# Attention block with a spiking feed-forward: another order for maxima, V, statistics, one relu and the last tokens

## The reference

```
mod = (silu(c) @ wmod) split into sa, ca, ga, sb, cb, gb      # one row per batch
h   = layernorm(x) * (1 + ca) + sa
q, k, v = split(h @ qkv_w.T + qkv_b)                           # 16 heads of 8
q, k = rope(q), rope(k)
attn = softmax(causal(q @ k.T / sqrt(8)))
x   = x + ga * ((attn @ v) @ proj_w.T + proj_b)
h   = layernorm(x) * (1 + cb) + sb
y   = square(relu(h @ W_fc.T)) @ W_proj.T                      # 128 -> 512 -> 128
x   = x + gb * (number of spikes of 5 leaky steps driven by y) / 5
```

## Time and profile before

| | |
|---|---|
| median of the runs | 450.79 us (449.61 to 452.21) |
| the profiled execution | 447.9 us, its span 446.1 us |
| TensorE busy (matmul) | 389.0 us, 87% of the span |
| VectorE busy | 320.0 us, 72% |
| ScalarE busy | 263.3 us, 59% |
| GpSimd busy | 125.4 us, 28% |
| maxima (L955) | 368 reductions, 192.2 us |
| exponentials (L809) | 288, 163.5 us |

### The profile page before, as it was taken

The page is one execution under the profiler, slowest core; times in us unless marked ns, Lnnn a source line. Parts: engine busy times, 40 slices in busy tenths (PEclk is TensorE's granted clock), DMA queues, the critical chain, the costliest instruction groups (busy, mean ns, idle before and its releaser), DMA issues.

```text
span 446.1 us, 15629 instructions
## 1 busy us (share of the span) xinstructions
PE 389.0 (87%) x6603; PEld 251.9 (56%) x6603; DVE 320.0 (72%) x718; ACT 263.3 (59%) x459; POOL 125.4 (28%) x163
## 2 busy tenths in 40 slices
PE   3878989878999999998999989999999889888883
PEld 3326655545656665666557655666566646654653
DVE  6659987857884999478965998489956875631275
ACT  7203556576677666765686657766676558467522
POOL 7714211421341052403250244205340320040120
PEclk9989999999999999999999999999999999999999
DMA  6056463242424332232414241323224040011000
GB/s 212 24 159 168 110 203 107 67 128 70 113 60 114 77 101 79 92 95 49 137 62 133 54 135 60 110 62 96 79 82 106 25 137 17 16 38 28 3 24 25
DMA packets 26049, 38.53 MB, mean 86 GB/s; under 512 B 5796, under 2 KB 20716, under 8 KB 23692
## 3 DMA queue, kind: packets, MB, share of 16 engines
q1 hardware_dynamic: 25980, 37.53, 29.3%
HBM read 26.35 MB, written 8.65 MB: 78 GB/s over the span
## 4 chain that ended last, share of the span: by engine, by line
PE 42%; DVE 18%; DMA 12%; issue 9%; ACT 8%; SPq 6%; POOL 5%; ACTq 0%; POOLq 0%; DVEq 0%
PE o_bank L606 9%; PE d_bank L523 8%; PE t_bank L588 6%; DVE negmax L955 6%; PE s_bank L543 5%; DMA kf<-k_scr 3%; SPq L440 3%; ACT probs L809 3%; DVE xn L971 3%; PE a_bank L523 2%; DMA rden<-r_scr 2%; DMA r_scr<-rden_c 2%; DMA den<-o_raw 2%; PE t_bank L523 2%; SPq L444 2%
## 5 line engine op out<-in xcount | busy, mean ns | idle before, releaser
L955 DVE TENSOR_REDUCE negmax<-s_bank 128x1 f32<-128x512 f32 (+7 forms) x368 | 192.2, 565 | 66.3 <-PE s_bank L549 65.0
L809 ACT ACTIVATE probs<-t_bank 128x512 f32<-128x512 f32 x288 | 163.5, 595 | 87.5 <-PE t_bank L593 83.1
L543 PE MATMUL s_bank<-kf,qf 126*64 126x512 bf16 (+7 forms) x1024 | 118.5, 292 | 18.3 <-DVE negmax L955 15.4
L588 PE MATMUL t_bank<-qf,kf 128*64 128x512 bf16 (+7 forms) x1024 | 112.0, 288 | 10.2 <-ACT probs L809 8.9
L543 PEld LDWEIGHTS s_bank<-kf,qf 126*64 126x64 bf16 x1024 | 49.5, 109 | 50.4 <-DVE negmax L955 36.2
L606 PE MATMUL o_bank<-probs,v 128*32 128x512 f32 (+7 forms) x1024 | 75.2, 412 | 0.0
L549 PE MATMUL s_bank<-causal,identb 128*64 128x64 bf16 x1024 | 72.0, 194 | 0.0
L593 PE MATMUL t_bank<-causal_t,identb 128*64 128x64 bf16 x1024 | 64.4, 195 | 0.0
L588 PEld LDWEIGHTS t_bank<-qf,kf 128*64 128x64 bf16 x1024 | 41.2, 110 | 31.6 <-ACT probs L809 11.5
L593 PEld LDWEIGHTS t_bank<-causal_t,identb 128*64 128x64 bf16 x1024 | 47.6, 110 | 9.2
L549 PEld LDWEIGHTS s_bank<-causal,identb 128*64 128x64 bf16 x1024 | 46.6, 111 | 8.3 <-issue 8.2
(11 more groups left out here) (144 smaller groups left out, 441.6 us busy)
## 6 DMA issues: line engine op xcount, KB each, us to landing
qf<-q_scr SPq DMA_DIRECT2D x15, 576.0 KB
kf<-k_scr SPq DMA_DIRECT2D x45, 192.0 KB
q_scr<-parts SPq DMA_DIRECT2D x24, 128.0 KB, 1.7
k_scr<-parts SPq DMA_DIRECT2D x24, 128.0 KB, 1.7
xa<-in_x SPq DMA_DIRECT2D x8, 256.0 KB, 3.8
o_t<-o_raw SPq DMA_DIRECT2D x60, 32.0 KB, 2.2
rden<-r_scr SPq DMA_DIRECT2D x15, 128.0 KB
out_y<-count SPq DMA_DIRECT2D x7, 256.0 KB, 7.2
```

Of the source, the lines that this page charges most:

```text
L543: nc.tensor.matmul(bank[C * a:C * (a + 1), col:col + keys], qf[0:KS, slot, 2 * p + a, C * i:C * (i + 1)], kf[0:KS, slot, 2 * p + a, 0:keys ...
L588: nc.tensor.matmul(bank[C * a:C * (a + 1), col:col + w], kf[0:KX, slot, 2 * p + a, C * kb:C * (kb + 1)], qf[0:KX, slot, 2 * p + a, C * kb: ...
L809: nc.scalar.activation(probs[:, v, :], t_bank[u % 2][:, :], ACT.Exp, scale=SCALE).then_inc(e_done, 1)
L955: last = nc.vector.tensor_reduce(own[:, i, p:p + len(same)], cols, AX.X, ALU.max, negate=True)
```

## The change

Nothing is computed differently; operations stand in other places of the engines' lists.

- The maxima follow the table S_PACE, which repeats in each batch: two units in slots 0, 1, 27, 29, 32 and 34, one in all others. The sum of a batch (42) and the lead are as before.
- V of the next batch is made in slot 5 and copied in slot 6, not in 0 and 1.
- Statistics of the inputs move from slot 13 to slot 0, their normalisation from 17 to 3, and GpSimd's `deviation1` ahead of the split of half 2b + 1.
- In slot 32 ScalarE does the relu before the copy of the maxima's rows.
- At the end the token blocks are paired (0, 2) and (1, 3) instead of (0, 1) and (2, 3), so the first reciprocal needs 128 columns of all partitions and not 256; the products of the second pair come after the first residual. The first half's down projection begins before the second half's up projections are done, and ScalarE alternates relu and square for the second half.

```diff
--- before.py
+++ after.py
@@ -37,6 +37,8 @@
 RING = 3
 HALF = SEQ // 2
 
+LAST_TOKENS = ((0, 2), (1, 3))
+
 
 S_BANKS = []
 for first in (0, 2):
@@ -68,6 +70,9 @@
 S_START = 22
 S_RISE = 2
 
+S_PACE = [2, 2, 1, 1, 1, 1] + [1] * 21 + [2, 1, 2, 1] + [1, 2, 1, 2, 1]
+S_DONE = [sum(S_PACE[:at + 1]) for at in range(PER_BATCH)]
+
 
 
 PV_ORDER = (0, 1, 7, 2, 6, 3, 5, 4)
@@ -85,7 +90,7 @@
 Q_STORES = NPART
 
 
-A_AT = {-16: T1, -13: QK, -9: QK + 1, 0: V_}
+A_AT = {-16: T1, -13: QK, -9: QK + 1, 5: V_}
 
 D_AT = {16: PROJ, 25: T2, 27: FC, 29: FC + 1, 31: FC + 2, 33: FC + 3}
 Y_AT = {36: 0, 37: 1, 38: 2, 39: 3}
@@ -97,7 +102,8 @@
 
 
 def scores_ahead(u):
-    return min(NS * HALVES, -(-(u + 1) * NS // NU) + S_LEAD, S_START + S_RISE * (u + 1))
+    b, at = divmod(u, PER_BATCH)
+    return min(NS * HALVES, 2 * NS * b + S_DONE[at] + S_LEAD, S_START + S_RISE * (u + 1))
 
 
 def bank_at(u):
@@ -510,7 +516,7 @@
             store_out(final - 1)
             for part in range(2):
                 sp.wait_ge(last_y, part + 1)
-                sp.dma_start(out_t[final, :, 2 * part:2 * part + 2], y_last[:, 2 * part:2 * part + 2, :])\
+                sp.dma_start(out_t[final, :, part:NT:2], y_last[:, 2 * part:2 * part + 2, :])\
                     .then_inc(stored, 16)
             sp.wait_ge(stored, 16 * (NB + 1))
 
@@ -767,10 +773,10 @@
             pe.wait_ge(on_done, NB)
             pe.wait_ge(wo_gated, NB)
             for part in range(2):
-                pe.wait_ge(last_on, part + 1)
-                for t in (2 * part, 2 * part + 1):
-                    cols = slice(P * t, P * (t + 1))
-                    last = by_halves(last_projected[part], cols, o_n[:, cols], wo_g[:, final % 2, :])
+                pe.wait_ge(last_on, 2 * part + 2)
+                for j, t in enumerate(LAST_TOKENS[part]):
+                    last = by_halves(last_projected[part], slice(P * j, P * (j + 1)), o_n[:, P * t:P * (t + 1)],
+                                     wo_g[:, final % 2, :])
                 last.then_inc(last_proj, 1)
 
             pe.wait_ge(m_free, rows_made(HALVES - 1))
@@ -782,22 +788,34 @@
                     last = nc.tensor.transpose(last_turned[part][:, P * t:P * (t + 1)], xn2[:, t, :], ident[:, :])
                 last.then_inc(last_t2, 1)
                 keep_warm(t_bank[1], 256)
-            for part in range(2):
-                pe.wait_ge(last_h2, part + 1)
-                cols = slice(HALF * part, HALF * (part + 1))
-                for i in range(NF):
-                    if part == 1 and i == NF - 1:
-
-                        pe.wait_ge(last_relu, 2)
-                    by_halves(last_hidden[part][i], slice(0, HALF), wfc_sb[:, P * i:P * (i + 1)], h2T[:, cols])                        .then_inc(last_fc, 1)
-            for part in range(2):
-                for i in range(NF):
-                    pe.wait_ge(last_sq[part], i + 1)
-                    for t in (2 * part, 2 * part + 1):
-                        cols = slice(P * t, P * (t + 1))
-                        last = by_halves(last_results[part], cols, sq[:, i, cols], wpr_sb[:, i, :],
-                                         i == 0 and t == 2 * part, i == NF - 1 and t == 2 * part + 1)
-                last.then_inc(last_out, 1)
+
+            def last_up(part, i):
+                by_halves(last_hidden[part][i], slice(0, HALF), wfc_sb[:, P * i:P * (i + 1)],
+                          h2T[:, HALF * part:HALF * (part + 1)]).then_inc(last_fc, 1)
+
+            def last_down(part, i):
+                pe.wait_ge(last_sq[part], i + 1)
+                for t in (2 * part, 2 * part + 1):
+                    cols = slice(P * t, P * (t + 1))
+                    last = by_halves(last_results[part], cols, sq[:, i, cols], wpr_sb[:, i, :],
+                                     i == 0 and t == 2 * part, i == NF - 1 and t == 2 * part + 1)
+                if i == NF - 1:
+                    last.then_inc(last_out, 1)
+
+            pe.wait_ge(last_h2, 1)
+            for i in range(NF):
+                last_up(0, i)
+            last_down(0, 0)
+            pe.wait_ge(last_h2, 2)
+            last_up(1, 0)
+            for i in range(1, NF):
+                last_down(0, i)
+
+            pe.wait_ge(last_relu, 2)
+            for i in range(1, NF):
+                last_up(1, i)
+            for i in range(NF):
+                last_down(1, i)
 
         @block.scalar
         def _(act):
@@ -902,20 +920,23 @@
             for u in range(SLOTS):
                 n, v = divmod(u, NU)
                 b, at = divmod(u, PER_BATCH)
+                relus, squares = (RELU_LAST, SQUARE_LAST) if b == final else (RELU_AT, SQUARE_AT)
+
+                if v == M_AT + 1 and at in relus and b > 0:
+                    hidden(b - 1, relus[at])
                 if u == M_SECOND + 1:
                     first_maxima_out(1)
                 if v == M_AT + 1 and n + 1 < HALVES:
                     maxima_out(n + 1)
                 if v == 3 and n > 0:
                     outputs(n - 1)
-                if at == 1 and 0 < b < final:
+                if at == 6 and 0 < b < final:
                     place_values(b + 1)
                 if at - PER_BATCH == -15 and b + 2 < NB:
                     modulate1(b + 2)
                 if at == (24 if b == final else 26) and b > 0:
                     modulate2(b - 1)
-                relus, squares = (RELU_LAST, SQUARE_LAST) if b == final else (RELU_AT, SQUARE_AT)
-                if at in relus and b > 0:
+                if v != M_AT + 1 and at in relus and b > 0:
                     hidden(b - 1, relus[at])
                 exponentials(u)
                 if at in squares and b > 0:
@@ -934,10 +955,11 @@
                 cols = slice(HALF * part, HALF * (part + 1))
                 for i in range(NF):
                     act.wait_ge(last_fc, NF * part + i + 1)
-                    nc.scalar.activation(relu[:, i, cols], last_hidden[part][i][:, 0:HALF], ACT.Relu).then_inc(last_relu, 1)
-            for i in range(NF):
-                act.wait_ge(last_relu, NF + i + 1)
-                nc.scalar.activation(sq[:, i, HALF:SEQ], relu[:, i, HALF:SEQ], ACT.Square).then_inc(last_sq[1], 1)
+                    nc.scalar.activation(relu[:, i, cols], last_hidden[part][i][:, 0:HALF], ACT.Relu)\
+                        .then_inc(last_relu, 1)
+                    if part:
+                        act.wait_ge(last_relu, NF + i + 1)
+                        nc.scalar.activation(sq[:, i, cols], relu[:, i, cols], ACT.Square).then_inc(last_sq[1], 1)
 
         @block.vector
         def _(dve):
@@ -1121,9 +1143,9 @@
             for u in range(SLOTS):
                 b, at = divmod(u, PER_BATCH)
                 if b + 2 < NB:
-                    if at - PER_BATCH == -23:
+                    if at == 0:
                         statistics1(b + 2)
-                    if at - PER_BATCH == -19:
+                    if at == 3:
                         normalise1(b + 2)
                     if at - PER_BATCH in ROTARY_AT:
                         rotary(b + 2, *ROTARY_AT[at - PER_BATCH])
@@ -1151,24 +1173,31 @@
 
 
             parts_of = [(slice(HALF * part, HALF * (part + 1)), slice(2 * part, 2 * part + 2)) for part in range(2)]
+            inverse = rot_c[:, 0, 0:HALF]
             sums, raw = last_sums[:, 0:HALF], last_rows[:, 0:HALF]
-            inverse = rot_c[:, 0, 0:HALF]
-            dve.wait_ge(gathered, 1)
-            nc.vector.reciprocal(inverse, sums).then_inc(last_rden, 1)
             dve.wait_ge(on_done, final)
             dve.wait_ge(d_ready, before(final - 1, PROJ) + 1)
-            dve.wait_ge(gathered, 2)
-            dve.wait_ge(last_rden, 1)
-            for part, (cols, _) in enumerate(parts_of):
-                own = slice(C * part, C * (part + 1))
-                nc.vector.tensor_tensor(o_n[C:P, cols], raw[own, :], inverse[own, :], ALU.mult).then_inc(last_on, 1)
+
+            def last_inverse(part):
+                dve.wait_ge(gathered, 1)
+                own = slice(P * part, P * (part + 1))
+                nc.vector.reciprocal(inverse[:, own], sums[:, own]).then_inc(last_rden, 1)
+
+            def last_outputs(part):
+                dve.wait_ge(gathered, 2)
+                dve.wait_ge(last_rden, part + 1)
+                for j, t in enumerate(LAST_TOKENS[part]):
+                    own, of = slice(C * j, C * (j + 1)), slice(P * part, P * (part + 1))
+                    nc.vector.tensor_tensor(o_n[C:P, P * t:P * (t + 1)], raw[own, of], inverse[own, of], ALU.mult)\
+                        .then_inc(last_on, 1)
 
             def last_residual(part):
                 cols, t2 = parts_of[part]
                 dve.wait_ge(last_proj, part + 1)
                 dve.wait_ge(xr_done, NB)
-                nc.vector.tensor_tensor(x1_last[:, t2, :], last_projected[part][:, cols].rearrange("p (t d) -> p t d", d=D),
-                                        xr[:, t2, :], ALU.add).then_inc(last_x1, 1)
```

(11 more changed lines are left out.)

## The result

The changed kernel takes 469.26 us (median; 466.74 to 473.17) where the kernel before takes 451.5 us beside it: the ratio is 1.040 (95% interval 1.035 to 1.046), 17.8 us by the medians. It is slower; the forecast was 444.5 us, with a range of 440.0 to 452.5. Every ratio in this document is against the kernel before as measured beside that run; a few executions that fell in a slower state are in the medians and not in the ratios. The profiled execution took 470.2 us, of which 468.2 are span.

The account below looks back on a forecast made before the run. TensorE was taken as the bound, working 44.83 us of a 48.30 us batch. Terms -6.0 (batches 2 to 5) - 0.8 - 1.2 + 1.5 + 0.2 = -6.3 gave 444.5 us from 450.8; range 440.0 to 452.5, by bounds 440.5 to 449.

Parts of the forecast that it names:

- A: Slots 0 to 16: moved V, first statistics and even pace relieve VectorE; gain 0.8 us a batch, bounds 0.3 and 1.05.
- B: Slots 13 to 27: normalisation moved to slot 3 and fewer maxima relieve VectorE; gain 1.0 us a batch, bounds 0.5 and 1.34.
- Step C: Slots 27 to 35: later GpSimd split delays K's cast and eats the relu swap's gain; net loss 0.3 us a batch.
- Slower: the split in GpSimd's queue: Rival: split at slot 28 delays K and ScalarE, reaching the next half's scores; 453 to 458 us, chance 0.10.
- D: Other batches: batch 6 gains 0.8 us, batch 7 1.2; batches 0 and 1 lose net 1.5, bounds 0.3 and 3.
- E: Program end: second residual 1.15 us later, first counts 1.3 earlier, 1.0 surviving; net loss 0.2 us, bounds -1.0 and +1.0.

Follow-up runs that it names:

- even-pace experiment: Changed kernel with the even table of the kernel before, all other parts of the change kept: 448.8 us, ratio 0.997.
- the table alone: Kernel before with the uneven table S_PACE and nothing else: 470.48 us, ratio 1.042.
- first experiment: Changed kernel with VectorE's reciprocal of the first half of heads in slot 27, not 25: 446.08 us, ratio 0.987.
- end-order experiment: Changed kernel with the first half's reciprocal in slot 27 and the second pair of products ahead of the first residual at the end: 443.35 us, ratio 0.985.
- the store later: Changed kernel with the first half's denominators and outputs gathered before the results of the batch before the last are stored: 462.59 us, ratio 1.025.

## Why the prediction was wrong

**The step that failed: A and B, slots 17 to 27.** They counted VectorE's work (11.67 less 2.06 less 1.2) and took for granted that a less loaded VectorE serves TensorE earlier. The sum of work was right. The step didn't ask, of each instruction in that queue, whether what it waits for also comes earlier. The forecast had a gain of 1.0 us a batch there; what came is a gap of 1.0 to 3.6 us at slot 27. The reciprocal is in the queue; the list of waits of the kernel before has a row for it (10.1 us, 7 times, longest 3.0), and its arrival there, 5.82 us after the gather's issue with 0.2 to 0.7 us to spare, could be read. The prediction named what stands behind a later instruction in GpSimd's queue (the split) and did not do the same for VectorE's.

**And what the table does to slot 27.** Step C followed the table to GpSimd's split in slot 28. It didn't follow it to the banks. One unit more by slot 27 means that TensorE asks for the reduction of slot 25, not of 24, and between the two stands the reciprocal. The even-pace experiment (9.5 us of waiting on VectorE for 11.3, gaps of 4.3 us there for 17.9) shows that this is the half that turns a wait into a loss, and the table alone that it is enough for a loss of its own.

**No term for the clock.** Every duration was taken at full clock. 10 to 11 us of the loss is the same work at half clock.

**A and B without the stall.** In the first experiment batches 2 to 5 take 189.9 us, before 193.2: 0.8 a batch, with 47.2 us in three of them. Forecast: 1.5, and a batch of 46.8. The normalisation takes 1.11 us in slot 3 without waiting, as said; VectorE's first stretch holds 6.6 us of work for 4.33 (slots 0 to 5 alone, 6.6 for 3.7). So the sign held and the size was half. By parts, in batches 3 to 5 of that experiment: B's gaps (slots 16 to 25) are 0.46 to 0.95 us for 1.18 to 2.06, 0.4 to 1.6 less and 0.9 on the mean, as forecast (1.0). A's gaps (slots 6 to 15) are 0.92 to 1.02 us for 0.92 to 1.03: of the 0.8 nothing came. The waits for maxima are gone there, but waits for exponentials of 0.53 and 0.36 us stand in their place. The first is the copy of V that A called harmless ("nothing late depends on them before slot 13"). It holds up exponential 6, and the scores of slot 8 wait for that one. ScalarE and TensorE in batch 4 of the changed kernel:

```profile
254.28 1.19 ACT L856 COPY v<-a_bank 64x512 f32<-64x512 f32 x2 [0.28 <-PE a_bank L645]
255.49 2.35 ACT L827 ACTIVATE probs<-t_bank 128x512 f32<-128x512 f32 x4
...
256.14 0.41 PE L594 MATMUL t_bank<-qf,kf 128*64 128x384 bf16 x4 [0.53 <-ACT probs L827]
```

This is read from the rows; no run moved the copy. In batch 4 the projection also waits for GpSimd's product of the outputs, which the forecast had not; TensorE, after:

```profile
265.58 1.09 PE L529 MATMUL d_bank<-wo_g,o_n 128*64 128x128 f32 x16 [0.73 <-POOL o_n L1324]
```

**C's mechanism was right.** In the end-order experiment slot 27's exponential of batch 4 starts at 269.64, before at 269.33, so times compare as they stand. The split came at 274.49 (forecast 274.2), Q's rest at 274.99 (274.7), K's cast at 279.41 (279.15), the wait for the exponential was 0.86 us (about 1). Its price was about right: TensorE waits 0.35 us for the relu and 0.86 for the exponential, before 0.90 and 0.16, 0.15 more for a forecast of 0.3. What C had not is the 0.41 us at slot 27 that is left of the table's gap: all gaps of slots 26 to 35 are 1.62 to 1.94 us in batches 3 to 5 of the first experiment, before 1.05. "Slower: the split in GpSimd's queue" was the rival on the right side with the wrong place: moving GpSimd's work gave at most 4.5 us (443.35 to 438.83), not 18.

**D was too small.** Batches 0 and 1 take 94.8 us in the first experiment, before 89.6: 5.2 lost against 1.5 forecast (bound 3), of which 3.4 us at half clock (from 106.1 on) explain up to 1.7. With Q's rest ahead of the split they take 90.2. The cause named, the late split, has a part in it, its price was not right. Batch 6 won 1.6 (forecast 0.8).

**E: one term mis-sized.** From the first up projection to the first counts 4.13 us instead of 5.42, so 1.29 as forecast, and 0.92 survive to the end (1.0). The late second pair costs 2.3 us, not 1.15: the forecast moved VectorE's product but left out that the warming matmuls stand behind TensorE's wait and run at half clock. From batch 7's start to the end the net is 0.2 better; forecast 1.0 better (D's 1.2 less E's 0.2).

The range failed because the slower rival was bounded by a late split; nothing in it could reach 469. The range "by the bounds of A to E" is also not their sum: added up, they give 436 to 458, and 458 does not reach it either.

## What to carry to other kernels

Before an engine is relieved, go down its queue over the stretch and write beside each instruction what it waits for; one that arrives with little slack at data from a DMA can stop the queue as soon as the engine gets there earlier, and everything behind it with it. Then look which buffers the bottleneck engine asks for across that instruction: a wait placed behind the reductions that are needed soon cost almost nothing (2.00 us of idle time, 0.41 of gap), one of 2.57 us ahead of them cost 3.5 us and the clock. When the order of work is driven by a table, a change of pace by one unit changes which producer each consumer depends on, so recheck each pair, and not only the sums.

## What the runs showed of the hardware

TensorE's gaps at slot 27 in the changed kernel, with the table alone and with the store later: of fourteen between 1.95 and 4.3 us ten were followed by a granted clock of 0.5 for 3.4 or 6.8 us, and of the shorter ones one (1.59 us). In the changed kernel that cost 10 to 11 us where the added standing still cost 13.5. Sixteen unread matmuls in the gap (1.9 us) gave back 10 to 11 us a run and cost 13, which only paid because they lay in time that was lost anyway. A gather of four times 4 KB took 3.8 us from its first issue with no spread near it and up to 8.5 (first experiment, batch 4) behind 1.15 MB of spreads.
